# Graph network layers: where and how wide VectorE rewrites the edge destinations while the adjacency is built

## The reference

```python
agg = jax.ops.segment_sum(x[src], dst, num_segments=N_NODES)   # in layers 0, 1 and 2
out = layernorm(x + layer(x, agg))                             # after every layer
dst = minimum((6250 * uniform ** 2.0).astype(int32), 99999)    # sorted: many edges at low numbers
```

## Time and profile before

| | |
|---|---|
| median of three runs | 4230.29 us (4230.21 to 4234.32) |
| the profiled execution: its own time | 4232.93 us |
| the profiled execution: its span | 4231.2 us |
| busy in the span: TensorE matmul, VectorE, ScalarE, GpSimd | 83%, 71%, 52%, 37% |
| mean granted TensorE clock | 0.891 of full speed |

### The profile page before, as it was taken

How to read it: one execution, slowest core, us unless ns; L and a number is a source line. 1 busy time by engine, 2 the same in 40 slices (tenths; PEclk the granted TensorE clock), 3 DMA queues, 4 the chain that set the end, 5 groups by cost and what they waited for, 6 DMA issues and landing times. The chain is left out here.

```text
span 4231.2 us, 94148 instructions
## 1 busy us (share of the span) xinstructions
PE 3503.2 (83%) x20637; PEld 2391.9 (57%) x20638; DVE 2994.9 (71%) x11952; ACT 2188.8 (52%) x6957; POOL 1547.7 (37%) x1256
## 2 busy tenths in 40 slices
PE   5878882698889899995997898688888888888884
PEld 2377772333333344443445344588888888888873
DVE  8899987698888888885003002688888888787875
ACT  2178884266677788884002001455555555555544
POOL 0078874000000000001002001377777777777770
PEclk8855555699999999997999999899999999999996
DMA  2011113001111222221983885355555555555551
GB/s 49 1 11 15 15 17 84 10 35 44 62 70 79 88 97 96 96 90 65 328 303 131 313 304 189 123 151 153 153 151 151 150 150 149 149 150 149 151 147 41
DMA packets 276478, 498.31 MB, mean 118 GB/s; under 512 B 92441, under 2 KB 192944, under 8 KB 276256
## 3 DMA queue, kind: packets, MB, share of 16 engines
q1 hardware_dynamic: 209922, 347.11, 24.4%
q0 software_dynamic: 66336, 149.10, 13.0%
HBM read 391.18 MB, written 104.89 MB: 117 GB/s over the span
## 5 line engine op out<-in xcount | busy, mean ns | idle before, releaser
L1706 POOL DMA_INDIRECT xs<-edge_table,ea_row_stage x1088 | 1089.1, 1001 | 347.4 <-issue 326.1
L1257 PE MATMUL a_agg_ps<-a_adj_ring,parts 128*128 128x512 f16 (+1 forms) x2548 | 523.7, 369 | 46.1 <-DMA a_adj_ring<-adjacency 46.1
L1926 ACT ACTIVATE slot_dst<-ea_onehot,ea_mask 128x128 f32<-128x128 f16 x1632 | 535.7, 399 | 13.2
L1056 PE MATMUL ab_agg_ps<-ab_adj_stage,parts 128*128 128x512 f16 x1911 | 528.2, 387 | 0.0
L1880 PE MATMUL ea_psz<-parts,ea_onehot_t 128*128 x2176 | 309.2, 287 | 206.6 <-issue 188.5
L1920 ACT ACTIVATE ea_mask<-ea_dot,b 128x4 f32<-128x4 f32 x408 | 121.3, 297 | 676.6 <-DVE slot_src L1831 672.9
L441 POOL DMA_INDIRECT records<-both_parts,record_row x98 | 356.1, 3633 | 291.0 <-ACT both_parts L467 269.1
L1397 POOL TENSOR_TENSOR parts<-xs,parts 128x896 f16<-128x896 f32 x7 | 13.2, 1883 | 1225.1 <-ACT parts L1391 1225.1
L1891 PE MATMUL ea_psa<-xs,slot_dst 128*128 128x129 f32 x3264 | 438.6, 278 | 2.4 <-ACT slot_dst L1926 2.4
L1129 ACT ACTIVATE ab_src_off<-iota,ab_neg_src 128x128 f16<-128x128 f16 x712 | 282.2, 396 | 304.8 <-issue 141.2
L1257 PEld LDWEIGHTS a_agg_ps<-a_adj_ring,parts 128*128 128x128 f16 x2548 | 242.2, 98 | 327.8 <-DMA a_adj_ring<-adjacency 47.0
(11 more groups left out here) (391 smaller groups left out, 6455.8 us busy)
## 6 DMA issues: line engine op xcount, KB each, us to landing
a_adj_ring<-adjacency SPq DMA_DIRECT2D x182, 896.0 KB, 4.6
ea_low_rows<-low_rows SPq DMA_DIRECT2D x411, 128.0 KB
adjacency<-ab_adj_stage SPq DMA_DIRECT2D x91, 512.0 KB, 2.6
adjacency<-ab_adj_stage SPq DMA_DIRECT2D x91, 384.0 KB, 2.3
ea_near_rows<-near_rows SPq DMA_DIRECT2D x137, 128.0 KB
xs<-edge_table,ea_row_stage POOLq DMA_INDIRECT x1088
edge_table<-vx SPq DMA_DIRECT2D x12, 512.0 KB, 2.9
ea_row_stage<-row_columns SPq DMA_DIRECT2D x272, 2.0 KB, 1.8
```

The costliest lines, as they stand in the source:

```text
L1056: ins = nc.tensor.matmul(agg_ps[:, :], lhs(r, t), stage[:, k, :], start=start and r == 0, stop=stop and r == parts - 1)
L1257: ins = nc.tensor.matmul(ps[:, h, 0:width], lhs(r, t), ring[:, g % SLOTS, k * DB:k * DB + width], start=t == 0 and r == 0, stop=t == NT - ...
L1706: nc.gpsimd.indirect_dma_start(got[:, h, g, k, 0:ROW], None, m.table, bass.IndirectOffsetOnAxis(ap=row_s[:, h, g, k:k + 1], axis=0)).then_ ...
L1926: ins = nc.scalar.activation(hot_m[:, g, k, :], hot[:, h, g, :, k], ACT.Copy, scale=mask[:, g, k:k + 1])
```

## The change

VectorE rewrites only the 1,664 columns that hold edges, and does it at the top of a round, behind the load of the counts. To make the first round alike, it adds 512 once ahead of the loop; to make the wait alike, it raises the semaphore `s_hot_l[6]` once by hand, so that TensorE waits for one more there. At the end it adds 12 x 512 back.

```diff
                 nc.vector.tensor_scalar(neg_src[:, :], m.slot_src[:, :], -1.0, None, ALU.mult).then_inc(s_neg, 1)
+                cells = m.slot_dst[:, 0:SCP]
+                nc.vector.tensor_scalar(cells, cells, float(DB), None, ALU.add).then_inc(s_v, 1)
+                dve.sem_inc(s_hot_l[TG - 1], 1)
                 with dve.Fori(0, NB) as b:
                     row = {}
                     for g in range(NG):
                         if g % 2 or g == 0:
                             two_rows(dve, row, b * NG + (g + g % 2), g + g % 2)
+                        if g == 0:
+                            dve.wait_ge(s_hot_l[TG - 1], b * NG + 1)
+                            dve.wait_ge(s_v, b + 1)
+                            nc.vector.tensor_scalar(cells, cells, -float(DB), None, ALU.add).then_inc(s_v, 1)
+                            dve.wait_ge(s_v, b + 2)
...
-                    dve.wait_ge(s_hot_l[TG - 1], b * NG + NG)
-                    nc.vector.tensor_scalar(m.slot_dst[:, :], m.slot_dst[:, :], -float(DB), None, ALU.add).then_inc(s_v, 1)
-                    dve.wait_ge(s_v, b + 1)
-                nc.vector.tensor_scalar(m.slot_dst[:, :], m.slot_dst[:, :], float(NB * DB), None, ALU.add).then_inc(s_v, 1)
-                dve.wait_ge(s_v, NB + 1)
+                dve.wait_ge(s_hot_l[TG - 1], NB * NG + 1)
+                nc.vector.tensor_scalar(cells, cells, float((NB - 1) * DB), None, ALU.add).then_inc(s_v, 1)
+                dve.wait_ge(s_v, NB + 2)
...
-                        pe.wait_ge(s_hot_l[k], n)
+                        pe.wait_ge(s_hot_l[k], n + 1 if k == TG - 1 else n)
```

## The result

The changed kernel took 4210.07 us (median of 4 runs, 4208.29 to 4215.46) beside 4232.31 us (median of 4 runs, 4230.21 to 4238.99) for the kernel before: a ratio of 0.9947, 95% interval 0.9935 to 0.9960. That is faster by 0.53%, 22.2 us between the medians.

The account below looks back on a forecast made before the run. VectorE was taken to pace early rounds, TensorE late ones. Terms 13.5 + 7.4 + 3.6 - 2.3 = 22.2 us off the profiled 4232.93 gave 4210.7; the median, 2.6 us lower, 4208 us, range 4194 to 4222.

Parts of the forecast that it names:

- the rival with no overlap: At round ends, VectorE's sequencer does not run ahead over the jump: 5 us gained, 4225 us; chance 0.13.
- Width and the new wait: At each round end, the rewrite of 1,664 columns takes 1.03 us, not 1.89; the wait on its semaphore 0.2 us.
- L: At round ends, how long before its end VectorE's last hot is handed over: 2.0 us, with 1.0 and 3.6 as ends.
- Early rounds: Five round ends with many edges, paced by VectorE: 2.7 us gained at each, 13.5 us in all.
- S: VectorE's jump, load of the counts and first register work at a round end: 5.31 us early, 4.48 late.
- the clock stays as it is: At early round ends, TensorE still falls to 1.2 GHz after 3.7 us of idleness, 0.58 us a matmul.
- more overlap, and the clock holds: Rival: L of 3 to 3.6, TensorE idle 2.5 to 3 us at early ends; 4193 to 4199 us; chance 0.10.
- Late rounds: Seven round ends with few edges, paced by TensorE: gain cut by `agg_t` of ScalarE, 7.4 us in all.
- Clock in late rounds: Two late rounds restarting TensorE at 1.2 GHz keep the clock as gaps shrink to about 2.6 us: 3.6 us gained.
- The start: Ahead of the build's first hot, two narrow rewrites and a wait are new: 2.3 us lost.
- The end: The last rewrites run beside TensorE's closing matmuls, so narrower ones gain nothing.
- The rival of a second fetch: A fetch boundary between load and first hot costs 3.3 us per round end: 18 us slower, 4248 us; chance 0.04.

Follow-up runs that it names:

- the second profile: The changed kernel run once more, unedited, for another profile (also called the repeated one): 4209.53 us, ratio 0.9946.
- the gap filled: Ten zero-weight matmuls ahead of TensorE's jump, added to the changed kernel (4199.51 us), and to it with `agg_t` copied first and a cheaper start (4201.11 us).
- `agg_t` first: The changed kernel with ScalarE copying the finished sums before its own adjacency copies instead of among them: 4200.98 us, ratio 0.9931.

## Why the prediction held, step by step

The forecast of 4208 us lies 2.1 us from the median; "faster" is right, and the rival with no overlap (4225 us) is what putting the wait back makes of the kernel (0.9983). But that the sum fits so well is partly luck: two errors cancel. By the two profiles the early rounds gave 3.0 and 3.9 us more than forecast, the late rounds with their clock 6.9 and 3.7 us less (forecast 7.4 + 3.6 = 11.0), and the start cost 1.1 and 0.9 us less.

**Width and the new wait.** 1.03 us and 0.25, forecast 1.03 and 0.2. Right.

**L.** Forecast 2.0, measured 2.0 as the mean over twelve round ends, from the run with the wait put back: (55.1 - 30.9)/12. It is not even: 2.5 at the five early ends (mean idle 4.78 and 2.25 us), 1.65 at the seven late ones (4.46 and 2.81), and by the same subtraction 1.3 to 3.3 at single ends. The estimate of 1.8 to 2.3 us by the Trainium skill (Advanced Engine Details and Errata, Engine Queue Depths) holds the mean and neither group. A queue of 8 may be the cause all the same; no run varied what is queued.

**Early rounds.** Forecast 13.5, measured 16.5 (17.4 by the second profile), so this term was sized too small. The early stall fell from about 7.2 to 3.5 us, 3.7 and not 2.7: L is 0.5 larger there, and S is 0.5 shorter in the changed kernel (mean idle 5.28 before, 4.78 with the wait put back; the first two ends are as before, the other three 0.7 to 0.9 us shorter). Why, no run shows. The step "the clock stays as it is" failed as well: TensorE stood only 1.1 to 3.25 us at these ends, where 3.5 to 4 was forecast. That is what the rival "more overlap, and the clock holds" said of the early rounds, and in part it came true. Four of five first matmuls at these ends take 0.38 us, one 0.52, where all five took 0.58. Much of the slow stretch moved to the second group (1122, 1211, 1297, 1376 in this profile), so what the clock gives there was not separated from the stall.

**Late rounds.** The cap by `agg_t` is right: 1447.55 to 1789.19, six restarts in a row stand 0.24 us behind it. Forecast 7.4 us; with the drops of the clock counted out, 475.2 - 468.5 = 6.7 (7.3 if a drop before is priced at 1.6 as well). The gain sits where the sum put it: rounds 8, 10 and 12 without a drop go from 68.0, 67.2 and 67.9 to 67.4 us, round 13 from 68.1 to 65.2.

**Clock in late rounds.** This step failed: +3.6 forecast, by the rule that a gap shrunk to 2.6 us keeps the clock. The gaps shrank further, to 2.33 to 2.36, and the clock fell in four late rounds of the profiled execution, in two of the repeated one, two before. The term is -2.6 in the one profile (4.1 less 6.7) and +0.6 in the other (7.3 less 6.7), where +3.6 was forecast: its sign depends on the execution. I had read rows of gaps with and without a drop as a threshold; they were no threshold: gaps of one length lie on both sides. In nine kept traces late second groups restart after gaps of 2.2 to 2.4 us, 49 in all, and the clock fell at 24 of them, two to four in each trace. In the two traces with the gap filled (0.67 us or less) it fell in none of fourteen rounds. So the gap is needed, and the start of the group as such does not do it. Why one gap of 2.33 us brings a drop and the next does not stays open. None of my runs tested what sets the choice.

**The start.** The first hot started at 802.44, 4.15 us behind the start of `neg_src` instead of 1.95: 2.2 us, forecast 2.3. Yet the first round lost only 1.2 (1.4 in the second profile). Other traces place the rest: from the first hot to the last hot this round took 196.2, 196.4 and 195.2 us in the three traces with the kernel before's top of the round, and 195.2 to 196.7 us in six with the changed one's. So the microsecond is the spread between executions, and nothing speaks against a loss of 2.2.

**The end.** Outside the build the profiles differ by 2 us (3105.3 and 3107.2), and by -0.3 in the repeated one (3105.0): nothing, as forecast. The rival of a second fetch did not occur: the only idle time of VectorE in the build that its own instruction stream ends is the twelve at the top, and behind the rewrite it waits 0.25 us.

The sum by the repeated profile: the build is 23.3 us shorter (1125.94 to 1102.61). The forecast build gain was 22.2, made of 13.5, 7.4, 3.6 and -2.3; the first profile read 16.5, 4.1 and -1.2, the second 17.4, 7.3 and -1.4.

## What to carry to other kernels

Idle time with no releaser behind the last instruction of a loop can be, as here, the jump and the load. If the instruction that must wait for the work before it is moved behind the jump, the sequencer can jump while that work still runs; here a single wait on the wrong side of the branch was worth 15 us over 12 round ends. Then ask which engine's own jump or copy is next in line: here `agg_t` and TensorE's jump stand so close that removing one shows the other, and in five of the seven late rounds the narrow rewrite alone had already used up what there was to gain. Where a gap shows matmuls at 1.2 GHz in some rounds, take two profiles of the same code, look at several matmuls behind each restart, and don't read a threshold out of one.

## What the runs showed of the hardware

- TensorE restarts behind its jump back 4.7 to 5.0 us after VectorE's last hot of the first group (nine of twelve rounds of the kernel before), and 4.80 to 4.86 us after ScalarE's where that is later (`agg_t` first, five late rounds). It is not a constant: the first round of the changed kernel reads 5.2 and its last 4.25, and with ten more matmuls ahead of the jump it is 5.35 to 5.43 behind ScalarE's.
- VectorE's instruction stream runs ahead over a taken jump: its idle time at the jump is 1.65 us shorter in the mean of seven late round ends and 2.5 us in the mean of five early ones than with one wait ahead of the jump.
- TensorE's granted clock fell from 2.4 to 1.2 GHz at or just behind restarts after 2.33 to 2.36 us of idleness in four of the six late rounds with such a gap in one execution and two of six in another of the same kernel, cost 1.4 to 1.7 us each time, and fell in none of fourteen late rounds where matmuls with zero weights cut the idleness to 0.67 us or less.
